# Attention slots without projections, second lead and tails reordered; output weights split in halves; last expert batch gated early

## The reference, cut to what matters

```python
x = x + attn0(layernorm(x))      # 32 heads, 8 groups, causal softmax
x = x + lora_experts(layernorm(x))   # router, top 16 of 64 experts of rank 16
x = x + attn1(layernorm(x))      # q and k RMS-normed, a linear position bias
x = x + ffn(layernorm(x))        # 4-bit weights: W = code[q] * absmax
```

## Time and profile before

| what | value |
|---|---|
| median of three runs | 1887.03 us |
| profiled execution, its own time | 1888.79 us |
| its span, first to last instruction | 1887.1 us |
| TensorE busy (PE) | 1756.8 us, 93% |
| DVE, ACT, POOL busy | 70%, 47%, 41% |
| mean granted clock of TensorE | 0.971 of full speed |
| the chain that ended last, by engine | PE 72%, DVE 11%, issue 6%, ACT 5%, POOL 5%, DMA 1% |

### The profile page before, as it was taken

One profiled execution on the slowest core, in us unless ns is written; L12 is line 12 of the kernel. 1 busy time (PEld: TensorE's weight loads), 2 busy tenths in 40 slices (PEclk: granted clock), 3 DMA queues, 4 the chain that ended last, 5 costly groups with the idle time before them and its releaser, 6 DMA issues.

```text
span 1887.1 us, 28594 instructions
## 1 busy us (share of the span) xinstructions
PE 1756.8 (93%) x8784; PEld 1451.9 (77%) x8784; DVE 1327.2 (70%) x2330; ACT 877.9 (47%) x2285; POOL 773.5 (41%) x924
## 2 busy tenths in 40 slices
PE   5999999999999979986899999999999996889999
PEld 4787888888888758875688787878787885668887
DVE  5678888787887865324678777777777775655555
ACT  2466566566556443222344444444444443544543
POOL 4334435253353432224535363535454523244442
PEclk8999999999999998889899999999999998999999
DMA  3122222122122201001001010000000002012111
GB/s 117 40 73 67 78 64 86 50 89 78 44 78 78 98 1 56 1 1 31 31 12 45 17 39 28 28 28 28 28 28 28 23 0 68 12 56 77 57 56 45
DMA packets 47711, 87.77 MB, mean 47 GB/s; under 512 B 6576, under 2 KB 6576, under 8 KB 47536
## 3 DMA queue, kind: packets, MB, share of 16 engines
q1 hardware_dynamic: 47664, 87.19, 14.6%
HBM read 77.73 MB, written 9.44 MB: 46 GB/s over the span
## 4 chain that ended last, share of the span: by engine, by line
PE 72%; DVE 11%; issue 6%; ACT 5%; POOL 5%; DMA 1%; POOLq 0%; DVEq 0%; SPq 0%; ACTq 0%
PE ring L298 13%; PE ring L300 13%; PE ring L299 13%; PE scores L298 4%; PE scores L299 4%; PE scores L300 4%; PE turned L298 3%; PE turned L300 3%; PE turned L299 3%; PE scores L628 3%; PE turned L714 2%; DVE lv_early L529 2%; ACT p L734 1%; PE turned L707 1%; POOL wd_lo L547 1%
## 5 line engine op out<-in xcount | busy, mean ns | idle before, releaser
L298 PE MATMUL ring<-xt_hi,w_lo 128*128 128x512 f32 x768 | 306.9, 400 | 7.4 <-DVE k_raw L841 4.5
L300 PE MATMUL ring<-xt_hi,w_hi 128*128 128x512 f32 x768 | 305.7, 398 | 0.0
L299 PE MATMUL ring<-xt_lo,w_hi 128*128 128x512 f32 x768 | 305.6, 398 | 0.0
L725 ACT CAST pt_hi<-turned 128x512 fp32r<-128x512 f32 x192 | 100.8, 592 | 264.6 <-PE turned L707 263.5
L298 PE MATMUL ring<-wd_hi,ot_lo 128*128 128x512 f32 x512 | 208.8, 408 | 13.2 <-DVE ot_lo L825 7.5
L299 PE MATMUL ring<-wd_lo,ot_hi 128*128 128x512 f32 x512 | 203.4, 397 | 0.0
L300 PE MATMUL ring<-wd_hi,ot_hi 128*128 128x512 f32 x512 | 203.2, 397 | 0.0
L546 POOL TENSOR_SCALAR sq_hi<-sq 128x512 fp32r<-128x512 f32 x80 | 55.2, 690 | 300.2 <-ACT sq L751 300.2
L298 PEld LDWEIGHTS ring<-xt_hi,w_lo 128*128 128x128 f32 x768 | 146.5, 191 | 40.8 <-DVE k_raw L841 4.9
L300 PEld LDWEIGHTS ring<-xt_hi,w_hi 128*128 128x128 f32 x768 | 145.9, 190 | 35.1
L299 PEld LDWEIGHTS ring<-xt_lo,w_hi 128*128 128x128 f32 x768 | 146.3, 190 | 31.9
(11 more groups left out here) (221 smaller groups left out, 4444.9 us busy)
## 6 DMA issues: line engine op xcount, KB each, us to landing
w_raw<-w_attn_dram SPq DMA_DIRECT2D x96, 256.0 KB, 3.2
wd_raw<-w_dense_dram SPq DMA_DIRECT2D x64, 256.0 KB, 2.7
code_early<-codes_dram SPq DMA_DIRECT2D x28, 256.0 KB, 2.9
absmax_early<-absmax_dram SPq DMA_DIRECT2D x56, 128.0 KB, 3.2
kept_dram<-deq_early SPq DMA_DIRECT2D x28, 256.0 KB, 2.1
stage<-kept_dram SPq DMA_DIRECT2D x28, 256.0 KB, 2.7
code_late<-codes_dram SPq DMA_DIRECT2D x14, 256.0 KB, 2.7
absmax_late<-absmax_dram SPq DMA_DIRECT2D x28, 128.0 KB, 2.9
```

What stands on the lines that cost most here:

```text
L298: nc.tensor.matmul(o, l_lo, r_hi, start=start, stop=False)
L299: nc.tensor.matmul(o, l_hi, r_lo, start=False, stop=False)
L300: return nc.tensor.matmul(o, l_hi, r_hi, start=False, stop=stop)
L725: nc.scalar.copy(pt_hi[:, j, :, :], turned[:, j, :, :]).then_inc(s_pt_hi, 1)
```

## The change

In the second lead `xn` lies in the memory of `p1`, as `sumsq` shares that of `xn`; POOL splits the second attention's first output weights at `split_wd` and no more at its start; the next group's V weights are loaded and split at `w_next`. The SP store of `kept` follows `dq_value`. The core of the rest of the diff:

```diff
                     elif step == ("out", 1) and b == 0 and g is not GROUPS:
                         pool.wait_ge(s_ring_full, pool_ring.value())
-                        pool_split_wd(pool)
+                        pool_split_wd(pool, range(HEADS if rms else 2))
+                    elif step[0] == "wd_rest":
+                        pool_split_wd(pool, range(2, HEADS))
...
+                    elif step[0] == "w_next":
+                        pool.wait_ge(s_ring_full, pool_ring.value())
+                        pool_split_w(pool, step[1])
+                    elif step[0] == "split_wd":
+                        pool_split_wd(pool)
...
-                pool_split_wd(eng)
+                if layer == 0:
+                    pool_split_wd(eng)
...
-            s += [("norm_write", 1, "act"), ("out", 2), ("norm_turn", 1)] + gated(3) + norm_begin([2], "pool")
+            s += gated(3) + [("norm_write", 1, "act"), ("out", 2), ("norm_turn", 1)] + norm_begin([2], "pool")
...
-            gated_hi, gated_lo = (w[:, :, :].rearrange("p h d -> p (h d)").rearrange("p (c q) -> p c q", q=SEQ)
-                                  for w in (wd_hi, wd_lo))
+            gated = [tuple(w[:, :, :].rearrange("p h d -> p (h d)").rearrange("p (c q) -> p c q", q=SEQ)
+                           for w in (wd_hi, wd_lo))]
+            gated.append(tuple(sb(f"gated_{name}", [P, EC, SEQ], F32R, scope) for name in ("hi", "lo")))
...
                         if b and step[2] == 0:
                             eng.wait_ge(s_ring_full, out_at)
+                        if b == 1 and step[2] == 0:
+                            eng.wait_ge(s_split, 2 * UNITS + 1)
                         at = slice(2 * step[2], 2 * step[2] + 2)
-                        nc.scalar.copy(gated_hi[:, at, :], ranks[:, at, :]).then_inc(s_gated_hi, 1)
+                        nc.scalar.copy(gated[b % 2][0][:, at, :], ranks[:, at, :]).then_inc(s_gated_hi, 1)
```

More of the change, by code:

```diff
@@ L95, in alibi_slopes, with slot_steps @@
     return [float(np.float32(start * start ** i)) for i in range(GROUPS * HEADS)]
-def slot_steps(b, rms, projects, first=False):
+def slot_steps(b, rms):
     half = 0 if b in (1, 2) else 1
-    ahead = 0 if b == 0 else 1
     tiles = [K, Q0, Q1] if b in (1, 3) else [Q2, Q3, V]
[L104 to L144, removed]
-        s += [("ffn_hi", k) for k in (2 * b - 2, 2 * b - 1)] + [("ffn_lo", k) for k in (2 * b - 2, 2 * b - 1)]
[L146 to L154, removed]
@@ new lines, in slot_steps @@
+    t = [("tile", x, half, 0 if b == 0 else 1) for x in tiles]
+    roots = rms and b in (1, 3)
+    s = [("pt_split",)] + ([] if rms else [("dq_lines", 0)])
+    s += [("scores", 0), ("mask", 0), ("max", 0, 0)] + t[0:1] + [("max", 1, 0), ("exp", 0), ("normalise", 0)] + t[1:2]
+    s += [] if rms else [("exp", 1)]
+    s += [("q_rms_turn", 1 if b == 1 else 0)] if roots else []
+    s += [("pv",)] + ([("exp", 1)] if rms else [])
+    s += [("roots", 1 if b == 1 else 0)] if roots else []
+    s += [("k_rms", half)] if rms and tiles[0] == K else []
@@ new lines, in slot_steps, with first_slot_steps @@
+    s += t[2:3] + [("normalise", 1)] + ([] if rms else [("dq_lines", 1), ("dq_top", 0)]) + [("out", 0)]
+    s += [("v_turn", half)] if tiles[-1] == V else []
+    s += [("k_norm", 1 if b == 1 else 0)] if roots else []
+    s += [] if rms else [("dq_top", 1)]
+    if rms:
+        s += [("out", 1), ("q_rms", half, 0 if tiles[0] == K else 1)]
+    else:
+        s += [("out", 1), ("dq_value",), ("wd_rest",)] if b == 0 else [("dq_value",), ("out", 1)]
+    return s + [("transpose",)]
+def first_slot_steps(rms):
+    softmax = [[("scores", 0), ("mask", 0), ("max", 0, 0)], [("max", 1, 0), ("exp", 0), ("normalise", 0)], [("exp", 1)]]
+    if rms:
+        s = [("tile", Q1, 1, 0)] + softmax[0] + [("q_rms", 1, 0), ("tile", Q2, 1, 0)] + softmax[1]
+        s += [("tile", Q3, 1, 0)] + softmax[2] + [("normalise", 1), ("w_next", V), ("q_rms", 1, 1)]
+        return s + [("transpose",)]
+    s = softmax[0] + [("tile", Q2, 1, 0)] + softmax[1] + [("tile", Q3, 1, 0)] + softmax[2] + [("tile", V, 1, 0)]
+    return s + [("normalise", 1), ("v_turn", 1), ("dq_first",), ("transpose",)]
@@ new lines, in last_slot_steps @@
+def last_slot_steps(b, rms):
+    s = [("pt_split",)] + ([("scores", 0)] if b == 1 else [])
+    if rms and b == 1:
+        s += [("q_rms_turn", 1), ("roots", 1), ("pv",), ("k_norm", 1), ("mask", 0)]
+    else:
+        s += [("mask", 0), ("pv",)]
+    s += [("max", 0, 0), ("exp", 0), ("max", 1, 0)]
+    s += norm_begin([b - 2], "pool") if b >= 2 else []
+    s += [("normalise", 0), ("exp", 1), ("normalise", 1), ("out", 0)]
+    if rms and b in (1, 2):
+        s += [("ffn_hi", k) for k in (2 * b - 2, 2 * b - 1)] + [("ffn_lo", k) for k in (2 * b - 2, 2 * b - 1)]
+    s += [("norm_write", b - 2, "act")] if b >= 2 else []
+    s += [("out", 1)] + ([("scores", 1)] if b < 3 else [])
+    return s + ([("norm_turn", b - 2)] if b >= 2 else []) + [("transpose",)]
@@ L1028, in pool_split_w, with pool_split_wd @@
                         w_raw[:, X % 3, :].rearrange("p (c d) -> p c d", c=DC), s_w)
-        def pool_split_wd(pool):
-            for h in range(HEADS):
+        def pool_split_wd(pool, heads=range(HEADS)):
+            for h in heads:
                 if h % 2 == 0:
```

49 lines of the change are left out of this document (28 added, 21 removed).

## The result

| kernel | median us | runs |
|---|---|---|
| before, beside it | 1888.9 (1886.41 to 1893.95) | 5 |
| changed | 1895.88 (1893.39 to 1899.38) | 5 |

A forecast was written before the change was run, and what follows sets the result against it. TensorE, busy 93% of the span, was taken as the bound, with time lost only in its waits and low clock. Terms +3.5 + 8 - 5 - 14 - 3 = -10.5 gave a median of 1876.5 us, range 1864 to 1888.

The forecast's parts named there:

- Loop, +3.5 forecast: First attention's loop: `dq_value` behind two weight splits shifts ScalarE's chain, +0.6 us a turn, six turns; ends -6.6 and +7.
- Rival A: Loop: ScalarE's chain has unseen room, so 6.6 us go in place of +3.5; total 1866, chance 0.13.
- First attention's last slots, +8 forecast: Slots without projections and tail: slot 3 +4.5, slot 2 0, slot 1 +0.5, tail +2.4, clock 0.6; ends +4, +12.
- The count from E: Slot 3: from the end of `pt_lo`, LayerNorm statistics start 6.0 us later, behind mask, two `ot_lo` and maxima.
- A quieter POOL: First attention's slot 3: a guessed half microsecond saved, taken off the norm chain's cost to give +4.5.
- Rival B: Slots 3 and tails: norm chain is covered, so 14 us of cost are absent; total 1863, chance 0.12.
- Experts, -5 forecast: Gates of batch 3 ahead of `out` 2: wait of 3.5 us goes, half of 2.9 returns; ends -3.5, -7.
- Second lead, -14 forecast: Second lead with first slot: new order cuts waits, 1 to 2 us less at low clock; ends -4, -20.
- the list of small waits: Second lead and first slot: six waits of 1.2 to 3.6 us, 11 in all, in place of 23.8 idle.
- Rival D: Second lead: POOL and DVE exclude each other, -14 becomes +2; slower, total +5.5, 1892.5, chance 0.10.
- Rival C: Second lead: only K's wait goes, POOL's queue still paces squares; -4 in place of -14, 1886, chance 0.13.
- Second attention, -3 forecast: Last slots: slot 2 -9, slot 1 -1, slot 3 +4.5, tail +2.4; ends -10, +2.

The follow-up runs named there:

- Experiment 4: Changed kernel with the two VectorE instructions of each first-attention top given one SBUF input instead of two: 1887.64 us, ratio 0.9981 to the kernel before.
- experiment 1: Changed kernel with its loop part alone undone (`dq_value` ahead of `out` 1, all four weight splits behind it): 1892.52 us, ratio 1.0000 to the kernel before.
- experiment 2: Kernel before with the loop part of the change alone: 1899.89 us, ratio 1.0048.
- experiment 10: Changed kernel with old loop order (last turn: weight splits before `dq_value`), early statistics, second lead's weight splits behind Q1's and Q3's squares: 1870.48 us, ratio 0.9884.
- experiment 5: Changed kernel with LayerNorm statistics and root of slots 2, 3 and tails directly behind `pt_split` again: 1882.83 us, ratio 0.9949 to the kernel before.
- experiment 7: Changed kernel with the second lead's four weight splits two behind Q1's and two behind Q3's squares: 1894.55 us, ratio 1.0014 to the kernel before.
- experiment 11: Kernel of experiment 10 with last squares split ahead of Q2's and Q3's weights in second attention's first slot: 1862.88 us, ratio 0.9850 to the kernel before.
- experiment 9: Kernel before with the experts' part alone (batch 3's gates ahead of `out` 2, own buffers for odd batches): 1887.12 us, ratio 0.9977.
- experiment 8: Changed kernel with its second lead and first slot alone put back to the old order: 1907.26 us, ratio 1.0079 to the kernel before.

## Why the prediction was wrong

Each of the five terms had its sign right; the sum had it wrong, because three of them were too good by 6.7, 5.0 and 4.1 us, all the same way, and the slot behind the lead added 1.0.

**Loop, +3.5 forecast, +10.2 measured, above its upper end of 7.** The failed step is the size of the shift, 1.3 with up to 0.9 more where the second top meets the first weight split, and the value of +0.6 taken between +0.25 and +1.1. It was 2.8: the codes are centred 8.8 us behind `out` 1 in all six turns, in the kernel before 6.0 (6.7 in the first). Row and rule were both in the text: the earlier trace rows shows 2.13 and 2.30 us where the ops meet, and the Trainium skill, "SBUF — State Buffer", section "Who interferes with whom", says that the one that starts first holds the other off for its whole instruction. The trace agrees (2.14, 1.67 and 1.07 in one turn: each ends its own usual length, less 0.14, behind the end of the other engine's). I took the mean of "meets" and "doesn't", though the new order puts the split right behind `out` 1 in every turn, and the top is there in every turn. And I charged one path only. The same meeting delays DVE's add into x and `kt_lo`, each with a wait of its own. Experiment 4 gives the two shares: 2.5 us for the order, where the +0.25 a turn makes 1.5, and up to 7.7 for the meeting. Rival A (ScalarE's chain has room) is refuted by the loop's +10.2 and by experiments 1 and 2; its 6.6 us were 1.0 more than the waits of the earlier trace rows.

**First attention's last slots, +8 forecast, +13.0 measured.** The count from E was right (5.8 for 6.0, and slot 2 near 0), and slot 3 and the tail wait for `xn` as forecast. The failed steps are three smaller terms. Slot 1 cost +2.0 for +0.5: `out` 0 comes early and waited 4.9 us for the last weight split. With all four splits behind `dq_value` that wait was 8.2 (experiment 1), with all four ahead of it the slot took 19.9 (experiment 10), so half of the splits came too late. "A quieter POOL" did not come: the root took 5.7 us, in the kernel before 5.5; one of its steps (701.07, 1.26 us for 0.19) was held by DVE's `p` of 1.23. Third the clock, put at 0.6: behind the wait of 5.7 us the transposes and half of the `pv` ran at 0.50. In the tail E came 4.1 us behind the transposes instead of 3.3, and the statistics 5.1 behind E where I had 3.8; that is 2.1 of the +4.7. In five other executions with this list the statistics came 3.7 behind E and the tail took 14.7 to 14.8, which is +3.3 for +3.0. The second attention's tail gave +2.0 for +2.4. Rival B (the chain is covered) is refuted by experiment 5.

**Experts, -5 forecast, -5.5 measured,** with the split between wait and clock as written. Alone on the kernel before it gave 5.7 by the marks and 4 by the ratio (2 to 7).

**Second lead, -14 forecast, -9.9 measured,** and +1.0 in the slot behind, whose clock fell from 0.96 to 0.92. The failed step is the list of small waits, 11 us; TensorE's idle time there fell from 24.3 only to 18.3. Its largest miss is the term "2.4 (`k_norm`)": the wait was 4.45, because the roots took 7.9 us beside the weight splits; where they took 4.4 (experiment 7) it was 2.4. The last wait for squares was 4.5 for 3.6, in part for the weights split ahead of them (experiment 11). And the list left out waits of 3.1 us that the kernel before has and the new order keeps: for the issue at the start (1.45), ahead of `norm_turn` (1.3) and for x (0.3). The busy time fell by 4.0, from 54.8 to 50.8, where 1 to 2 were put for the clock, or the gain would have been smaller. Rival D had the mechanism and the place, and its total of 1892.5 came near the measured time; that is luck. Its price rested on stretched splits, which would have cost the lead its whole gain; POOL's splits kept their 1.3 us there, only DVE's small instructions were held, by 2.1 us on the path in `k_norm`, and the time was lost in other stages. Experiment 7 got 3.5 us back: 2.1 in `k_norm` and the wait of 1.1 for K's squares, which the forecast had counted. Rival C is refuted: the gain is more than twice its 4.

**Second attention, -3 forecast, -2.7 measured:** each slot within 1.2 us; the +5.6 of slot 3 for +4.5 and the -9.8 of slot 2 for -9 offset each other, which is in part luck.

All in all, the places were right and the sizes were not. VectorE and GpSimd shutting each other out accounts for the loop's miss and for about half of the lead's; in the last slots it is a late weight split and the low clock behind new waits. The ends of the terms, taken as independent, give 12 to 14 us to each side and not the 10 that the text says; and there was no reason to take them as independent, since two of them hang on the same meeting and erred the same way.

## What to carry to other kernels

Before work is moved on GpSimd, list what VectorE does in that window with SBUF operands, and where rows of the kernel show such instructions held (as the earlier trace rows did), charge the meeting in full in each turn in which both are there, on every path behind the delayed instruction; a chain of tiny VectorE steps pays much for little work (7.9 us for 4.4). When a reordering brings a consumer forward, ask at once when its inputs come (here `out` 0 against the weight splits, and the statistics against the transposes), and test the parts one by one: here losses of 9 to 10 and of 12 to 16 us hid gains which, with the weight splits and the last squares reordered as well, made the kernel 1.5% faster. And before one stage of two executions is compared, look at how much that stage differs between executions that have the same list: here the lead's 79.0 looked like an effect of the experts until that of experiment 2 was laid beside it.

## What the runs showed of the hardware

- A VectorE instruction of 20 columns took 1.16 us in place of 0.18 beside a GpSimd split of 1.31, and ended 0.04 us behind it; the next two of its kind took 1.13 and ended 0.05 and 0.03 behind the next two splits. The cost is what is left of the other's instruction, not a share of its own length. For longer ones too: a held instruction ended its own usual length, less some 0.14 us, behind the other's end (1.15 for a split of 1.29, 0.55 for a VectorE one of 0.69, 0.48 for a cast of 0.62).
- It goes both ways: a GpSimd instruction of 2 columns took 1.26 us in place of 0.19 beside a VectorE one of 1.23.
- A VectorE instruction with a single SBUF input is held too: L327, 0.40 us from 901.24, ends at 901.64, where POOL's `wd_hi` (901.00, 0.62) ends at 901.62. One of 128x1024 took 1.78 us for 0.68 and ended 0.55 behind a split (experiment 4).
- The same list of steps, with waits that were longer by 0.3 us at most, took 79.0, 81.0, 82.1 and 82.3 us in four kernels (before, experiments 9, 8 and 2), at granted clocks of 0.88, 0.84, 0.83 and 0.83. The order of the experts ahead of it doesn't sort them: 79.0 and 82.3 have the old one. The slot behind it, without a wait, took 23.5, 23.6, 22.8 and 22.8.
- Behind a wait of 5.7 us TensorE ran at a granted clock of 0.50 for 8.6 us, with matmuls of 512 columns starting 0.43 us apart in place of 0.23.
